# GRU step of a graph network kernel: which TensorE matmuls stand ahead of the waits for the state's two halves

## What is computed

```
pre_i = x_seq @ W_ih.T + b_ih
def step(h, pi):
    ph = h @ W_hh.T + b_hh
    r = sigmoid(pi[:H] + ph[:H])
    z = sigmoid(pi[H:2*H] + ph[H:2*H])
    n = tanh(pi[2*H:] + r * ph[2*H:])
    h_new = (1.0 - z) * n + z * h
    return (h_new, h_new)
_, ys = jax.lax.scan(step, h0, pre_i)      # 1250 steps, H = 512
```

## The kernel before

| slots before | matmuls | ahead of them |
|---|---|---|
| 0-3 | r of half 0 from state half 0, low weights | wait: high part of state half 0 (`gru_state0`, 2t+1), and `gru_put0` |
| 4-7 | the same, high weights | wait: low part of state half 0 (`gru_state0`, 2t+2) |
| 8-23 | z, then n, of half 0 from state half 0 | |
| 24-31 | r of half 1 from state half 0 | `gru_put1`, 3t+1 |
| 32-35 | n of half 1 from state half 0, first two pieces | `gru_put1`, 3t+2 |
| 36-39 | r of half 0 from state half 1, low weights | wait: high part of state half 1 |
| 40-43 | the same, high weights; slot 43 tells `gru_r_mm0` | wait: low part of state half 1 |
| 44-59 | z, then n, of half 0 from state half 1 | |
| 60-67 | r of half 1 from state half 1 | |
| 68-71 | n of half 1 from state half 0, last two pieces | |
| 72-79 | n of half 1 from state half 1 | |
| 80-95 | z of half 1 from both halves; slot 95 tells `gru_z_mm1` | `gru_put1`, 3t+3 |

## Time and profile before

### The profile page before, as it was taken

The page is one execution under the profiler, slowest core; times in us unless marked ns, Lnnn a source line. Parts: engine busy times, 40 slices in busy tenths (PEclk is TensorE's granted clock), DMA queues, the critical chain, the costliest instruction groups (busy, mean ns, idle before and its releaser), DMA issues.

```text
span 5286.2 us, 338777 instructions
## 1 busy us (share of the span) xinstructions
PE 5071.3 (96%) x128234; PEld 4262.3 (81%) x128235; DVE 3006.4 (57%) x16450; ACT 2112.3 (40%) x15422; POOL 943.4 (18%) x5221
## 2 busy tenths in 40 slices
PE   5669999999999999999999999999999999999989
PEld 4555559999999999999999999999999645555654
DVE  6662336666666666666666666666666444355551
ACT  0110005555555555555555555555555201221110
POOL 1230002222222222222222222222222100000000
PEclk8559999999999999999999999999999998999989
DMA  1002220000000000000000000000000100001011
GB/s 59 0 3 97 80 87 0 0 0 0 0 0 0 0 0 0 0 0 0 0 0 0 0 0 0 0 0 0 0 0 0 54 8 10 35 35 35 19 46 45
DMA packets 28930, 81.07 MB, mean 15 GB/s; under 512 B 1594, under 2 KB 1834, under 8 KB 28858
## 3 DMA queue, kind: packets, MB, share of 16 engines
q1 hardware_dynamic: 28858, 80.03, 4.1%
HBM read 58.08 MB, written 21.95 MB: 15 GB/s over the span
## 4 chain that ended last, share of the span: by engine, by line
PE 92%; DVE 3%; issue 3%; DVEq 2%; ACT 0%; POOL 0%; DMA 0%; SPq 0%; POOLq 0%; ACTq 0%
PE psum L501 63%; PE psum L570 8%; PE psum L376 5%; PE psum L366 4%; PE psum L582 4%; PE psum L483 2%; PE psum L556 2%; PE psum L646 1%; PE psum L423 1%; DVE r L879 1%; DVEq L874 1%; DVE r L878 1%; DVEq L872 1%; DVEq L871 1%; PE psum L433 0%
## 5 line engine op out<-in xcount | busy, mean ns | idle before, releaser
L501 PE MATMUL psum<-h,r 128*128 128x16 f16 (+1 forms) x80000 | 3063.4, 181 | 11.1 <-ACT psum L706 4.4
L501 PEld LDWEIGHTS psum<-h,r 128*128 128x128 f16 x80000 | 2544.2, 96 | 113.0 <-ACT psum L706 5.0
L501 PE MATMUL psum<-h,hn 128*128 128x16 f16 (+1 forms) x40000 | 1801.3, 178 | 0.0
L501 PEld LDWEIGHTS psum<-h,hn 128*128 128x128 f16 x40000 | 1416.5, 96 | 0.0
L997 DVE TENSOR_TENSOR_SCAN psum<-mul_rz,psum 128x6 f32<-128x6 f32 x5000 | 871.6, 174 | 611.9 <-PE psum L501 563.1
L706 ACT COPY psum<-big 128x2 f32 (+1 forms) x7506 | 1002.8, 163 | 0.0
L328 POOL TENSOR_TENSOR upd_add<-upd,signs 128x4 f32<-128x4 f32 x2500 | 499.4, 200 | 2708.0 <-DVE h L1014 1524.0
L719 ACT ACTIVATE mul_n<-psum 128x2 f32<-128x2 f32 x2500 | 434.4, 174 | 1197.8 <-DVE psum L997 1197.8
L1011 DVE TENSOR_TENSOR_SCAN upd<-upd_mul,upd_add 128x8 f32<-128x8 f32 x2500 | 437.1, 175 | 414.1 <-ACT upd_mul L724 299.3
L728 ACT ACTIVATE upd_add<-psum 128x2 f32<-128x2 f32 x2500 | 433.4, 173 | 254.3 <-DVE psum L1003 238.7
L1003 DVE TENSOR_TENSOR_SCAN psum<-mul_n,psum 128x8 f32<-128x8 f32 x2500 | 446.8, 179 | 112.6
(11 more groups left out here) (231 smaller groups left out, 2791.2 us busy)
## 6 DMA issues: line engine op xcount, KB each, us to landing
ws<-in_Wl SPq DMA_DIRECT2D x9, 1024.0 KB, 5.3
ws<-in_Wr SPq DMA_DIRECT2D x9, 1024.0 KB, 7.7
edge_counts<-adj SPq DMA_DIRECT2D x2, 3051.8 KB
edge_weights<-big SPq DMA_DIRECT2D x1, 6103.5 KB
adj_rows<-big SPq DMA_DIRECT2D x1, 6103.5 KB
adj<-adj_rows SPq DMA_DIRECT2D x1, 6103.5 KB
big<-edge_counts SPq DMA_DIRECT2D x1, 6103.5 KB
adj<-edge_weights SPq DMA_DIRECT2D x1, 6103.5 KB
```

The lines of the kernel that those rows point to most:

```text
L501: m = mm(places, whh16[g][:, part, 2 * kc + k, (2 * c + j) * P:(2 * c + j + 1) * P], state.unsqueeze(1).broadcast_to([P, COPIES, 2 - part] ...
```

## The change

The change reorders TensorE's instructions within a step. No instruction is added or removed, no other engine's order changes, and the waits are the same in number and in value. Two moves are made:

- The low weights of z for half 0 from state half 0 (four matmuls) go ahead of the wait for the low part of state half 0.
- The first two pieces of n of half 1 from state half 0 (four matmuls), with the wait for the second `gru_put1`, go from ahead of the waits for state half 1 to behind slot group r of half 1, beside the other two pieces.

```
                     pe.wait_ge(s("gru_state0"), 2 * t + 1)
                     pe.wait_ge(s("gru_put0"), t + 1)
-                    gru_gate(u, 0, 0, 0, part=1)
+                    for g in (0, 1):
+                        gru_gate(u, 0, 0, g, part=1)
                     pe.wait_ge(s("gru_state0"), 2 * t + 2)
-                    gru_gate(u, 0, 0, 0, part=0)
-                    for g in (1, 2):
-                        gru_gate(u, 0, 0, g)
+                    for g in (0, 1):
+                        gru_gate(u, 0, 0, g, part=0)
+                    gru_gate(u, 0, 0, 2)
                     pe.wait_ge(s("gru_put1"), 3 * t + 1)
                     gru_gate(u, 1, 0, 0)
-                    pe.wait_ge(s("gru_put1"), 3 * t + 2)
-                    gru_gate(u, 1, 0, 2, every[:2])
                     pe.wait_ge(s("gru_state1"), 2 * t + 1)
...
                     gru_gate(u, 1, 1, 0).then_inc(s("gru_r_mm1"), 1)
-                    gru_gate(u, 1, 0, 2, every[2:])
+                    pe.wait_ge(s("gru_put1"), 3 * t + 2)
+                    gru_gate(u, 1, 0, 2)
                     gru_gate(u, 1, 1, 2).then_inc(s("gru_n_mm1"), 1)
```

## The result

| | before | changed | ratio (95% interval) |
|---|---|---|---|
| median of timed executions | 5285.2 us (5 runs, 5269.1 to 5293.7) | 5319.3 us (5 runs, 5315.6 to 5326.6) | 1.0069 (1.0048 to 1.0089) |
| profiled execution (span) | 5288.3 us (5286.2) | 5315.6 us (5313.2) | |

The changed kernel is 0.7% slower: 34 us by the medians, 36 by the ratio. The forecast was 5308 us and 0.6%, against a median before of 5277.5 us, which two more executions have moved to 5285.2.

The account below looks back on a forecast made before the run. Before, TensorE's matmul flow plus waits for state half 0 makes a 2.686 us step. After, half 1's loop takes 1.16 + 1.54 + 0.01 = 2.71 us; 1250 x 0.024 = 30 us more gives 5308 us, range 5285 to 5325.

Parts of the forecast that it names:

- Free flow of 0.026 us a slot, waiting only at half 0: TensorE before: 96 matmul slots a step would take 2.51 us unhindered; 0.18 us is waiting, all for state half 0.
- Slot 0 at about Z + 0.04 in steps within a pass: First matmul of a step: with half 0's arithmetic four slots earlier, it starts there instead of at Z + 0.14.
- Z: Start of slot 95, the last matmul of a step on TensorE; times in the next step count from it.
- Nothing in half 1's chain from Z to L1020 is pushed: ACT and DVE work on half 1: each begins 0.03 to 0.04 us after its input; 0.93 us as before.
- The rival in which DVE's queue frees the scan of z: DVE, half 1: z's scan starts up to 0.10 us earlier, 58 us less, 5220 us; chance 5%.
- Slot 36 waits until Z + 1.16: Wait for half 1's low part: high weights can start 0.06 us behind L1020's end; slot 40 had 0.07 us of cover.
- Every step is held there, so what the first move saves goes into this wait: Slot 36: reached unhindered at Z + 0.99 or Z + 1.15, both before Z + 1.16, so the saving at slot 0 is lost.
- The rival of late steps past Z + 0.21: Steps at the start of a pass begin at, say, Z + 0.25: 55 us more, 5333 us; chance 4%.
- The size: Whole GRU loop: step of 2.71 us against a mean of 2.686, 0.024 us more, 30 us over 1250 steps.
- the 1.54: Time in us from slot 36 to slot 95 of one step, 59 slots of 0.0261 each.
- The refill: Behind the wait at slot 36: the weight load starts only when the state is there, adding 0.01 us a step.
- the 18 us that were weighed by the rule: Sum instead of 30 us if slot 36's weight load passed the wait and the 0.01 us of refill fell away.

Follow-up runs that it names:

- e1: Only the first move, made on the kernel before; n of half 1 stays where it was: 5251.2 us, ratio 0.9950.
- e2: Only the second move, made on the kernel before; the start of the step stays as it was: 5324.2 us, ratio 1.0087.
- e4: Changed kernel, with z's low weights for half 0 from state half 1 also ahead of the wait for half 1's low part: 5236.4 us, ratio 0.9929.
- e8: Changed kernel with four steps instead of two in a pass of TensorE's loop: ratio 1.0063.
- e3: Changed kernel, but one piece of n (two matmuls) stays ahead of the waits for state half 1: ratio 0.9992; run again on another chip, 0.9951.
- e10: e4 with one matmul of n back ahead of the waits for state half 1: 5239.9 us, ratio 0.9902.
- e11: e4 with four steps in a pass and one matmul of n back ahead of the waits for half 1: 5217.1 us, ratio 0.9864.

## Why the prediction was right

- **Free flow of 0.026 us a slot, waiting only at half 0.** Held. e1 took part of this waiting away and gained 31 us in the loop.
- **Slot 0 at about Z + 0.04 in steps within a pass.** It is Z + 0.03 (2501.30 against 2501.27).
- **Nothing in half 1's chain from Z to L1020 is pushed.** Held: 0.93 us both times. The rival in which DVE's queue frees the scan of z falls with the row at Z + 0.23.
- **Slot 36 waits until Z + 1.16.** Held to the last digit, in the changed kernel and in e2. The prediction gave no time for the wait for the high part at slot 32, which is a second gap, of some 0.07 us. It costs nothing here, as slot 36 waits afterwards all the same; in e4 it becomes the bound.
- **Every step is held there, so what the first move saves goes into this wait.** Shown by e2, which lacks the first move and has the same loop within 3 us, and by e8, where fewer jumps bring nothing. The rival of late steps past Z + 0.21 didn't occur; e2's late steps, with slot 0 at Z + 0.20, come to its very edge.
- **The size.** The step was put at 2.71 us and measured 2.722. From slot 36 to the next slot 95 it took 2503.99 - 2502.43 = 1.56 us, not 1.55: the first spacing behind the wait is 0.039 us where flow is 0.026, so it adds 0.013 and not 0.01, and the 1.54 was a difference of two rounded starts. 0.036 us instead of 0.024 make 45 us instead of 30 in the loop. The medians moved by 34 and the ratio says 36, within its interval of 25 to 47. The time of 5319 us lies 11 above the forecast; 8 of these come from the median before, 5285.2 instead of 5277.5 us, and the medians moved 11 us less than the loops, which the 19 us that the rest of the program varies between traces can hide. A term read to 0.01 us is worth 12 us here, and that was the uncertain part, as the text had it.
- **The refill.** The weight load of slot 36 starts with its matmul, 0.05 us behind the end of L1020:

```profile
2502.42 0.11 PEld L501 LDWEIGHTS psum<-h,r 128*128 128x128 f16 x2
```

The Trainium skill (page "TensorE: Matmul & The Clock Gate", section "Step-by-step: what each phase is for") says that TensorE's queue pulls weight loads ahead of matmuls in flight. Of waits this sentence says nothing; in this kernel the load doesn't pass the wait, and the 18 us that were weighed by the rule would have been further off than 30.

- **Wrong in the expectations behind the prediction.** e3's late starts, more than one slot of room at half 0 for e10, and, by far, the ten steps in a pass.

## What to carry to other kernels

Where a serial loop has more than one ring of dependences, moving work ahead of one wait takes it from the cover of another: work out for each wait how long its input takes from the signal that starts it, and how many slots lie between. A step is as long as its longest ring, and a saving in a shorter one is worth nothing, as here 31 us. When TensorE runs chains of short matmuls its busy time shows none of this; count starts and look at the spacing.

## What the runs showed of the hardware that was not expected

- A loop body of ten steps on TensorE, 1920 weight loads and matmuls, was fetched anew in each pass: 1302 instruction packets and 21.3 MB instead of 55 and 0.9, idle stretches of 4.47 us, and 23% more time. A body of four steps, 768 loads and matmuls, some 68 KB by the estimate of 17 KB a step from e8, stayed at 59 packets. The bound lies between; it was not searched.
- Behind the jump of TensorE's loop the first matmul comes at Z + 0.15 or Z + 0.20 although its state is there; the share of the later one is about a half before, in e4, in e8 and in e11, a third in e1 and e10, five in six in e2, and none or almost none in the changed kernel and in both traces of e3's kernel. Where the jump is the bound it is worth up to 625 x 0.046 = 29 us in the loop, so it enters differences between loops such as e1 against e3. What decides it stays open.
